# Norm, turned rows and router logits of layer 1's experts moved into the cross attention's program

## What is computed

```python
x = x + _L0_attn_ref(_layernorm(x), ...)           # causal attention
x = x + _L0_xattn_ref(_layernorm(x), ctx_1024, ...) # gated MLP on the context
x = x + _L0_ffn_ref(_layernorm(x), ...)            # shared and routed experts
x = x + _L1_attn_ref(_layernorm(x), ...)           # full attention, 16 heads of 16
x = x + _L1_xattn_ref(_layernorm(x), ctx_1024, ...) # cross attention
x = x + _L1_ffn_ref(_layernorm(x), ...)            # 8 experts, top 2
```

```python
logits = x @ gate_w.T                               # x: the norm, 2048 x 256; gate_w: 8 x 256
routing_weights, selected = phi_routing(logits)     # top 2 of 8, masked softmax
for e in range(E):
    h = silu(x @ w1[e].T) * (x @ w3[e].T)
    out = out + wte[:, e:e + 1] * (h @ w2[e].T)
```

## Time and profile before

| | us |
|---|---|
| median of 3 runs | 1841.25 (1840.33 to 1841.65) |
| the profiled execution, its own time | 1839.36 |
| its span in the profile | 1837.5 |
| PE busy | 1551.0 (84%) |
| DVE busy | 1210.9 (66%) |
| ACT busy | 928.3 (51%) |
| POOL busy | 575.4 (31%) |
| last add to x in l1a ends | 1327.4 |
| first choosing step of l1m begins | 1355.0 |

### The profile page before, as it was taken

One profiled execution on the slowest core, in us unless ns is written; L12 is line 12 of the kernel. 1 busy time (PEld: TensorE's weight loads), 2 busy tenths in 40 slices (PEclk: granted clock), 3 DMA queues, 4 the chain that ended last, 5 costly groups with the idle time before them and its releaser, 6 DMA issues. The chain is left out here.

```text
span 1837.5 us, 32551 instructions
## 1 busy us (share of the span) xinstructions
PE 1551.0 (84%) x11264; PEld 1113.0 (61%) x11264; DVE 1210.9 (66%) x1994; ACT 928.3 (51%) x1746; POOL 575.4 (31%) x785
## 2 busy tenths in 40 slices
PE   4889896878999995688888887887655999999996
PEld 2445453568999994333333332332254999999995
DVE  3665552556788883777767366777666777777773
ACT  1345443133366662254645556667613666666662
POOL 5344520010155554634434321010001333333321
PEclk8899998989999997699999987997856999999998
DMA  5222210121278894421212212222034777767763
GB/s 141 45 50 54 51 39 24 57 92 64 81 219 236 232 226 122 95 47 36 55 39 54 63 35 59 45 57 48 13 126 132 207 204 207 218 192 225 200 179 86
DMA packets 192834, 200.21 MB, mean 109 GB/s; under 512 B 33121, under 2 KB 167778, under 8 KB 192642
## 3 DMA queue, kind: packets, MB, share of 16 engines
q1 hardware_dynamic: 161186, 159.85, 29.6%
q0 software_dynamic: 31488, 38.31, 11.1%
...
## 5 line engine op out<-in xcount | busy, mean ns | idle before, releaser
L1740 PE MATMUL l1m_g_ps<-l1m_sb_rows_hi,l1m_sb_hi 128*128 128x256 f32 x736 | 210.8, 286 | 10.9 <-DVE l1m_sb_late L1639 9.5
L673 ACT ACTIVATE l1a_sb_probs<-l1a_s_ps,l1a_sb_kmax 128x512 f32<-128x512 f32 x256 | 172.4, 706 | 75.4 <-issue 60.3
L1740 PE MATMUL l1m_g_ps<-l1m_sb_rows_hi,l1m_sb_lo 128*128 128x256 f32 x736 | 210.4, 286 | 0.0
L1740 PE MATMUL l1m_g_ps<-l1m_sb_rows_lo,l1m_sb_hi 128*128 128x256 f32 x736 | 210.2, 286 | 0.0
L586 DVE TENSOR_REDUCE l1a_sb_mx<-l1a_s_ps 128x2 f32<-128x1024 f32 x128 | 154.1, 1219 | 65.0 <-PE l1a_s_ps L758 65.0
L620 DVE TENSOR_REDUCE l1a_sb_kmax<-l1a_s_ps 128x2 f32<-128x1024 f32 x128 | 154.1, 1216 | 48.9 <-PE l1a_s_ps L795 48.2
L679 ACT ACTIVATE l1a_sb_probs<-l1a_s_ps 128x1024 f32<-128x1024 f32 x128 | 128.1, 1022 | 91.3 <-PE l1a_s_ps L795 90.9
L586 DVE TENSOR_REDUCE l0a_sb_mx<-l0a_s_ps 128x2 f32<-128x256 f32 (+3 forms) x128 | 103.5, 821 | 80.0 <-PE l0a_s_ps L769 78.6
L795 PEld LDWEIGHTS l1a_s_ps<-l1a_sb_qst,l1a_sb_kst 49*128 49x128 f32 (+1 forms) x512 | 50.9, 199 | 172.9 <-issue 89.9
L795 PE MATMUL l1a_s_ps<-l1a_sb_qst,l1a_sb_kst 49*128 49x512 f32 (+1 forms) x512 | 131.7, 521 | 26.7 <-ACT l1a_sb_probs L673 22.1
L1740 PEld LDWEIGHTS l1m_g_ps<-l1m_sb_rows_hi,l1m_sb_hi 128*128 128x128 f32 x736 | 143.3, 195 | 11.5 <-issue 9.7
...
## 6 DMA issues: line engine op xcount, KB each, us to landing
...
l1a_sb_qst<-l1a_sb_hi SPq DMA_DIRECT2D x256, 32.0 KB, 2.0
...
l0a_sb_qst<-l0a_sb_hi SPq DMA_DIRECT2D x128, 32.0 KB, 2.1
l0a_sb_kst<-l0a_sb_hi POOLq DMA_DIRECT2D x128, 32.0 KB, 2.0
```

The source lines that it names most:

```text
L673: ins = act.activation(probs[:, n % 8, e, :], at[:, e, :], ACT.Exp, bias=kmax[:, n % 4, e:e + 1], accum_out=zsum[:, n % 4, e:e + 1])
L1740: ins = pe.matmul(at, s, m, start=n == 0, stop=n == len(passes) - 1)
```

## The change

The norm, the turning and the logits leave the program l1m and come into l1a as five steps for each cross pass. RN1 is the statistics on DVE and the deviation on POOL. RN2 is the normalised rows on DVE (tile xr) and SP's store of them to DRAM. RT, twice, is four transposes of xr into `m_ps` and ACT's copy to xrT. RL is the logits into `m_ps` and ACT's copy of them to a tile in SBUF, from which `top1` now reads. For passes 4, 5 and 6 these steps stand in slots (5,3), (6,3) and (7,3): RN1 behind step j = 0, RN2 behind j = 1, RT behind j = 3 and j = 4, RL behind j = 6. For pass 7 they stand at the end of the program. The router's weights are loaded once more, at the start of l1a. The experts of layer 0 keep their own head.

```diff
@@ def attention_slot(kinds, b, g):
+    done = b - 1 if b and g == NG - 1 and kinds[b - 1] == "cross" else None
...
         if j < last_late and j == 0:
             yield "PV", *last, NT - 3
+        if done is not None and j in (0, 1):
+            yield ("RN1", "RN2")[j], done, 0, 0
+        if done is not None and j in (3, 4):
+            yield "RT", done, j - 3, 0
+        if done is not None and j == 6:
+            yield "RL", done, 0, 0
         if j == last_late and has_last:
             yield "PV", *last, NT - 2
@@ def attention_schedule(kinds):
     for j in range(2):
         yield "OUT", b, g, j
+    if kinds[b] == "cross":
+        yield "RN1", b, 0, 0
+        yield "RN2", b, 0, 0
+        yield "RT", b, 0, 0
+        yield "RT", b, 1, 0
+        yield "RL", b, 0, 0
@@ def attention(nc, tag, x, const, stages, router=None):
+        if router is not None:
+            rstats, rmv, rrstd = sb("rstats", [P, NT, 6]), sb("rmv", [P, NT, 2]), sb("rrstd", [P, 2, NT])
+            xr, xrT, rw = sb("xr", [P, NT, D]), sb("xrT", [P, CC, T]), sb("rw", [P, CC, E])
...
+            def store_rows(b, *_):
+                r_xn.wait(sp, b, NT - 1)
+                sp.dma_start(const["xn"][b % B * T:(b % B + 1) * T].rearrange("(t p) d -> p t d", p=P), xr[:, :, :]
+                             ).then_inc(const["xn_stored"], 16)
+
+            if router is not None:
+                sp.dma_start(rw[:, :, :], router.rearrange("(c p) e -> p c e", p=P)).then_inc(router_in, 16)
+            run({"STACK": stack, "LN1": before_batch, "M": rows, "RN2": store_rows})
...
+            def deviation(b, *_):
+                r_stats.wait(pool, b, 2 * NT - 1)
+                if b % B:
+                    r_xn.wait(pool, b - 1, NT - 1)
+                pool.tensor_tensor(rrstd[:, 0, :], rmv[:, :, 1], const["eps"][:, :], ALU.add).then_inc(r_rstd.sem, 1)
+                r_rstd.wait(pool, b, 0)
+                pool.tensor_tensor(rrstd[:, 1, :], rrstd[:, 0, :], const["minus_half"][:, :], ALU.pow
+                                   ).then_inc(r_rstd.sem, 1)
...
+            def router_stats(b, *_):
+                x_added.wait(dve, b, NG - 1)
...
+                for t in range(NT):
+                    dve.bn_stats(rstats[:, t, :], x[:, b % B * NT + t, :]).then_inc(r_stats.sem, 1)
+                r_stats.wait(dve, b, NT - 1)
...
+                for t in range(NT):
+                    dve.bn_aggr(rmv[:, t, :], rstats[:, t, :]).then_inc(r_stats.sem, 1)
+
+            def router_rows(b, *_):
+                r_stats.wait(dve, b, 2 * NT - 1)
+                r_rstd.wait(dve, b, 1)
+
+                if b % B:
+                    r_turned.wait(dve, b - 1, CC - 1)
+                    dve.wait_ge(const["xn_stored"], b % B * 16)
+                for t in range(NT):
+                    dve.tensor_scalar(xr[:, t, :], x[:, b % B * NT + t, :], rmv[:, t, 0:1], rrstd[:, 1, t:t + 1],
+                                      ALU.subtract, ALU.mult).then_inc(r_xn.sem, 1)
...
+            def turned_rows(b, c, _):
+                r_turned.wait(act, b, c)
+                if b % B:
+                    r_logits.wait(act, b - 1, 0)
+                act.activation(xrT[:, c, :], m_ps[:, :], ACT.Copy).then_inc(r_copied.sem, 1)
+
+            def logits_out(b, *_):
+                r_logits.wait(act, b, 0)
+                act.activation(const["logits"][:, b % B * NT:(b % B + 1) * NT, :],
+                               m_ps[:, 0:NT * E].rearrange("p (t e) -> p t e", e=E), ACT.Copy).then_inc(r_read.sem, 1)
...
+            def router_turn(b, c, _):
+                r_xn.wait(pe, b, NT - 1)
+                take_m(r_copied, b, c)
+                for t in range(NT):
+                    ins = pe.transpose(m_ps[:, t * P:(t + 1) * P], xr[:, t, c * P:(c + 1) * P], const["ident"][:, :])
+                ins.then_inc(r_turned.sem, 1)
+
+            def router_logits(b, *_):
+                if b % B == 0:
+                    pe.wait_ge(router_in, 16)
+                r_copied.wait(pe, b, CC - 1)
+                take_m(r_read, b, 0)
+                for t in range(NT):
+                    for c in range(CC):
+                        ins = pe.matmul(m_ps[:, t * E:(t + 1) * E], xrT[:, c, t * P:(t + 1) * P], rw[:, c, :],
+                                        start=c == 0, stop=c == CC - 1)
+                ins.then_inc(r_logits.sem, 1)
@@ def moe_schedule(shared, nf):
     else:
-        yield "TURN", 1, 0
-        yield "LOGITS", 0, 0
...
-        yield "LOGITS", 2, 0
-        yield "LOGITS", 3, 0
+
         for step in ("TOP1", "TOP2", "RANK", "EXPERTS", "LOAD", "ROWS", "PLACES", "HELD"):
@@ def moe(nc, tag, x, const, w, width, phi, shared, out=None):
-        l_ps = y_ps[:, 1, :, :].rearrange("p t d -> p (t d)")[:, 0:NTILE * E].rearrange("p (t e) -> p t e", e=E)
+        logits_at = y_ps[:, 1, :, :].rearrange("p t d -> p (t d)")[:, 0:NTILE * E].rearrange("p (t e) -> p t e", e=E)
+        l_ps = logits_at if shared else const["logits"][:, :, :]
...
-                if not shared:
-
-                    sp.wait_ge(xn_stored, B * 16)
-                    xn_turned.wait(sp, B - 1, CC - 1)
@@ def route(dve, then, const, phi, weights_ps, at, sems):
     def top1(*_):
-        sems["logits_ready"].wait(dve, B - 1)
+        if not phi:
+            sems["logits_ready"].wait(dve, B - 1)
         dve.wait_ge(sems["router_in"], 32)
@@ def build(nc, inputs, out):
-        attention(nc, "l1a", x, const, [("full", of("l1a")), ("cross", of("l1x") | context)])
+        attention(nc, "l1a", x, const, [("full", of("l1a")), ("cross", of("l1x") | context)],
+                  inputs["l1m_router"])
```

More of the change, by code:

```diff
@@ L202, in attention_schedule, with attention @@
         yield "OUT", b, g, j
-def attention(nc, tag, x, const, stages):
+    if kinds[b] == "cross":
[4 more added lines that the diff above has]
+        yield "RL", b, 0, 0
+def attention(nc, tag, x, const, stages, router=None):
     kinds = [kind for kind, _ in stages for _ in range(B)]
@@ L320, in attention @@
         ox_copied = steps("ox_copied", 0, NG // 2)
+        router_in = sem("router_in")
+        r_stats, r_rstd, r_xn = steps("r_stats", 0, 2 * NT), steps("r_rstd", 0, 2), steps("r_xn", 0, NT)
+        r_turned, r_copied = steps("r_turned", 0, CC), steps("r_copied", 0, CC)
+        r_logits, r_read = steps("r_logits", 0, 1), steps("r_read", 0, 1)
         def first_col(kt):
@@ L435, in _ @@
                              ).then_inc(ones_in, 16)
-            run({"STACK": stack, "LN1": before_batch, "M": rows})
+            def store_rows(b, *_):
[5 more added lines that the diff above has]
+            run({"STACK": stack, "LN1": before_batch, "M": rows, "RN2": store_rows})
         @block.gpsimd
@@ L510, in scale_v @@
                                    ALU.mult).then_inc(v_scaled.sem, 1)
-            run({"LN1": ln, "LN2": bias, "STACK": stack, "V": v_group, "W": scale_v})
+            def deviation(b, *_):
[6 more added lines that the diff above has]
+                                   ).then_inc(r_rstd.sem, 1)
+            run({"LN1": ln, "LN2": bias, "STACK": stack, "V": v_group, "W": scale_v, "RN1": deviation})
         @block.vector
@@ L629, in inverse_sums @@
                 dve.reciprocal(rzsum[:, w % 2, :, :], zsum[:, n % 4:n % 4 + 2, :]).then_inc(rz_done.sem, 1)
-            run({"LN1": ln, "LN2": normal, "PREP": prep, "LO": rest, "OUT": out, "S": key_max, "W": inverse_sums,
+            def router_stats(b, *_):
+                x_added.wait(dve, b, NG - 1)
+                if b % B:
+                    r_stats.wait(dve, b - 1, 2 * NT - 1)
+                for t in range(NT):
+                    dve.bn_stats(rstats[:, t, :], x[:, b % B * NT + t, :]).then_inc(r_stats.sem, 1)
+                r_stats.wait(dve, b, NT - 1)
+                if b % B:
+                    r_rstd.wait(dve, b - 1, 1)
+                    r_xn.wait(dve, b - 1, NT - 1)
+                dve.memset(nothing[:, :], 0.0)
+                for t in range(NT):
[3 more added lines that the diff above has]
+                r_rstd.wait(dve, b, 1)
+                if b % B:
+                    r_turned.wait(dve, b - 1, CC - 1)
[3 more added lines that the diff above has]
+                                      ALU.subtract, ALU.mult).then_inc(r_xn.sem, 1)
+            run({"RN1": router_stats, "RN2": router_rows, "LN1": ln, "LN2": normal, "PREP": prep, "LO": rest, "OUT": out, "S": key_max, "W": inverse_sums,
                  "A": row_max, "Z": invert})
@@ L848, in project @@
                 ins.then_inc(out_ready.sem, 1)
+            def router_turn(b, c, _):
[14 more added lines that the diff above has]
+                ins.then_inc(r_logits.sem, 1)
             run({"PREP": prep, "S": scores_by_key, "PV": probs_v, "OUT": project, "A": scores_by_query,
-                 "M": max_rows, "Z": turn, "N": turn_back})
+                 "M": max_rows, "Z": turn, "N": turn_back, "RT": router_turn, "RL": router_logits})
```

(23 more changed lines are left out.)

10 lines of the change are left out of this document (3 added, 7 removed).

## The result

| | before | after |
|---|---|---|
| median, both timed side by side, us | 1840.33 (1838.38 to 1841.65, 5 runs) | 1855.24 (1849.03 to 1857.78, 5 runs) |
| ratio, 95% interval | | 1.0085 (1.0070 to 1.0101) |
| span of the profiled execution | 1837.5 | 1853.4 |
| last add to x in l1a ends | 1327.4 | 1353.5 |
| first choosing step of l1m begins | 1355.0 | 1370.6 |

The change makes the kernel 0.85% slower. The forecast was 1852.6 us, 0.6% slower. The head shrank as meant, and the attention grew by more than that.

A forecast was written before the change was run, and what follows sets the result against it. The prediction took a chain of waits as the bound, with DVE and ACT nearly full in slot (5,3). 1839.36 + 22.6 for the slots - 11.2 from the head = 1850.8; with 1.9 to the median, 1852.6 us, range 1839 to 1864.

The forecast's parts named there:

- Head gives back 11.2: Last add in l1a to first choosing step in l1m: shrinks from 27.7 to 16.5 us, giving back 11.2.
- six terms: Parts left in the head: norm 4.9, turning 3.6, logits 3.5, ACT's logits copy 0.3, barrier 1.2, bias wait 3.0 us.
- k1 and k2: Starts of the maxima of steps 1 and 2, counted from step 0's in each changed slot: 2.9 and 5.7 us.
- The wait for step 5: In each changed slot, PE's second transposes wait for ACT's first copy, delaying step 5's scores; its maximum starts at 14.1 us.
- k5: Start of the maximum of step 5, counted from step 0's in each changed slot: 14.1 us.
- My signs: Trace signs expected in the changed slots, among them DVE waiting 2 to 4 us for the scores of step 5.
- From k5 to k7: From the maximum of step 5 to that of step 7 in each changed slot: 3.4 us, TensorE at 2.4 GHz.
- The other end: From the maximum of step 5 to that of step 7, TensorE at 1.2 GHz: 6.8 us, kept for the range.
- Hidden copies, only DVE counts: Rival: in the slots copies and PE's waits hide, three slots cost 9.1 us; 1839.2 to 1836.5 us; chance 0.13.
- TensorE stays fast: Rival: TensorE at 2.4 GHz, a slot 18.2 us, cost 16.9, head gives 13.9; 1844.3 us; chance 0.20.
- TensorE slow through the whole slot: Rival: TensorE at 1.2 GHz in the changed slots, a slot 23.5 us, cost 32.8; 1862.9 us; chance 0.15.
- Second bank: Another PSUM bank for the turned halves: step 5's maximum at 11.2 not 14.1, 8.7 us less in three slots.

The follow-up runs named there:

- Norm only: Changed kernel without the transposes and logits of the first three batches, the slots keeping only the norm and the store; 1838.79 us, ratio 1.0007 to the kernel before.
- spread: Changed kernel with ACT's copies behind steps 2 and 4, transposes behind steps 3 and 5, logits behind step 7; 1849.77 us, ratio 1.0062 to the kernel before.
- the second measurement: The changed kernel again, unedited, against the kernel before; 1852.78 us, ratio 1.0078.

## Why the prediction was right, and where it was off

- **Head gives back 11.2.** It gave 10.6. All six terms hold within 0.7. The one most in doubt, the new wait for the bias, was real: it is named in the trace, and taking it away shortened the head by 3.6.
- **Norm in the slot, k1 and k2.** 2.9 and 5.7 predicted, 2.87 and 5.71 to 5.74 measured. Slot (6,0), where the kernel already did the same for another purpose, was a price list good to 1%.
- **The wait for step 5.** k5 14.1 predicted, 14.14 to 14.17 measured. Norm only and spread show the cause: without the transposes, or with ACT's copy early and the second half later, k5 is 9.2 to 10.3. The wait in DVE is 4.89. My signs said 2 to 4, which my own sum contradicts: the maximum of step 4 ends at 9.3, and 14.1 - 9.3 is 4.8. I had taken 1.2 GHz for everything up to k5; slot (5,3) turned the first half at 2.4 GHz (0.66 us, where the other two took 1.11 and 1.12), and k5 was the same, since ACT's queue and not TensorE set the time of the copy.
- **From k5 to k7, the step that failed.** I took 3.4, at 2.4 GHz, on the argument that PE has work without a gap once the copy is there. Measured: 3.64, 6.53 and 6.53. The work was without a gap, and the argument failed all the same: in slot (6,3) TensorE was busy 7.66 of the 7.70 us from 1268.40 on, at PEclk 0.50. The other end, 6.8 at 1.2 GHz, had the size right, but I had made it all or nothing for the three slots and given it 0.15. Two of three were slow in this trace, one of three in the second. Each slow one costs 2.9, and two of them are 5.8 of the 6.7 us by which the slots' cost of 29.3 passed the predicted 22.6; the rest is a few tenths a slot in the exponentials at the end.
- **Why the forecast still came near.** Its sum was +11.4. With 6.7 more in the slots and 0.6 less from the head it would have been +18.7; 4.1 of drift ahead of slot (5,3), which no step of mine contained, brought the two profiled executions to +14.6, and 1.3 lie elsewhere. So 1852.6 is nearer to 1855.2 than its steps were to theirs, and that is luck. The medians differ by 14.9, and by 14.5 in the second measurement. What makes them some 4 us less than +18.7 is open: there is one trace of the kernel before, and slots that no edit touches have two lengths in the traces, (7,1) 10.1 or 11.8 and (6,0) 23.9 or 25.5.
- **The rivals.** *Hidden copies, only DVE counts* falls: the copy stood behind the exponentials of step 3. *TensorE stays fast* falls: what k5 hangs on, the second transposes and the product, ran at 1.2 GHz in all three slots, and so did the head. *TensorE slow through the whole slot* is half true: it fits two slots of three, with 23.3 measured for its 23.5. The Trainium skill (TensorE: Matmul & The Clock Gate, section HAM oscillation) has waits between groups of matmuls throttle TensorE to half each time anew, if they are long enough. Slot (5,3) fits that, 1.09 for the transposes behind the wait of 3.49 us and 0.66 for those behind 2.54. But the length alone doesn't settle it: in the kernel with the bias early, a wait of 2.54 ahead of the first transposes of slot (7,3) was followed by the lower level, 1.11.
- **Second bank.** The rule to rotate PSUM banks (the Trainium skill, Perfetto Trace Analysis, section Matmuls) was not tried, so the 11.2 that I had worked out for k5 stays untested. Spreading the two halves gives what the rule is after, a copy that runs under other work of TensorE, and k5 came to 9.2 to 10.3, below those 11.2.

What stays open: what decides the level between k5 and k7. No run changes that alone. But the level could be told before k5, from the first transposes, as the table in the last section has it.
